# Layer normalisation moved from VectorE to ScalarE in a four-layer decoder, with a new table of step order

## The chip, the cores and the metric

The kernel is one program on one core of a Trainium2 chip. The time is the device time of that core in microseconds. The engines are named as in the profile: PE is the matrix engine (TensorE), PEld its weight loads, DVE is VectorE, ACT is ScalarE, POOL is GpSimd, SP is SyncE, which issues most of the DMAs.

## The reference

The reference is a decoder of 4 layers over x of shape (4, 256, 128) in float32: 4 batch entries, 256 tokens, width 128. Each layer is attention of some kind, cross attention of some kind and a feed-forward part with 8 experts; behind each of the 12 comes

```python
def _layernorm(x, axis=-1, eps=1e-05):
    m = jnp.mean(x, axis=axis, keepdims=True)
    v = jnp.var(x, axis=axis, keepdims=True)
    return (x - m) / jnp.sqrt(v + eps)

x = _layernorm(x + _L0_attn_ref(...))      # a state space scan over the tokens
x = _layernorm(x + _L0_xattn_ref(...))
x = _layernorm(x + _L0_ffn_ref(...))       # attention, rmsnorm, experts, rmsnorm inside
x = _layernorm(x + _L1_attn_ref(...))      # ... and so on, 12 times
```

The first feed-forward part holds an attention and two RMS normalisations with a weight vector of its own. The third feed-forward part (L2) sends tokens to experts through memory; the attention of L3 is linear attention with a softmax feature map.

## The kernel before, in words

The program calls the 12 parts 13 sublayers (`SUBLAYERS`), since the attention inside the first feed-forward part counts by itself as `("attn", 1)`. A sublayer is worked through for each of the 4 batch entries b. A batch entry is 256 tokens, held as two tiles of 128 tokens on the partitions by 128 features (`x_tok`), and also transposed (`xT`, features on the partitions), which is what the matmuls read.

All work is cut into some 2,550 steps, such as ("SM", a, b, i), ("P2", a, b, i) or ("NORM", s, b). A step names what it does on each engine; the tuple `COST` and the function `cost` give the planner's figures for it. `lanes()` puts the steps in 49 lanes, each with a fixed order within itself. The string `ORDER` has one letter for each step and says from which lane the next step comes. `plan()` reads it, chooses the PSUM banks, and puts in filler matmuls (step FILL, line 1036, on the identity matrix) where its own figures leave PE waiting for long. Each engine then goes through the steps in this one order and issues its own part of each. An engine's instructions run in the order in which they were issued; semaphores join the engines. So a step whose input is late holds up everything behind it on that engine.

At the end of a sublayer stand, for each batch entry, these steps:

- STAT: DVE adds the residual into `res` (line 1804), takes mean and variance with two BATCH_NORM_STATS2 and two BATCH_NORM_AGGREGATE (lines 1726 and 1730) into `mv`; POOL adds epsilon to the variance (line 1679) and raises it to the power -0.5 (line 1680) into `rstd`. STAT2 is a second such step in the first expert sublayer.
- NORM: DVE waits for `rstd` and computes (res - mean) * rstd, one TENSOR_SCALAR for each of the two tiles (line 1833). In `("attn", 1)`, which is an RMS normalisation, it is `res * rstd * norm_w` (line 1831). DVE then waits for its own result.
- XT: PE transposes `x_tok` (line 1062), ACT copies it to `xT` (line 1381). Everything in the next sublayer for that batch entry reads this.

Other names: line 1774 is the scan of the first sublayer on DVE, line 1371 the exponentials that it reads (ACT), 1377 a copy (ACT), 1611 the product behind it (POOL). Line 1448 is the exponential of the softmax (ACT), 1875 the row maximum (DVE), 1701 a product on POOL in the linear attention, 2012 the product with the gates in the expert parts (DVE).

The 13 sublayers of the 4 batch entries overlap in the order. Read by the lines that run in them, the stretches are roughly: to 134 us the scan of the first sublayer, to 275 us the first two attentions, to 560 us the first experts, the wide self attention, a cross attention and the second experts, to 700 us the causal and masked attentions, to 850 us the dispatched experts, to 1000 us the linear attention, then the last cross attention and the last experts.

Of the kernel before, what the change touches and what calls it, by code (L numbers as in the profile page):

```python
# [62 lines left out]
    "STAT": ((DVE, 1.2), (POOL, 1.1)), "XB": ((POOL, 0.8),), "STAT2": ((DVE, 1.95), (POOL, 1.1)), "NORM": ((DVE, 0.62),), "XT": ((PE, 0.22), (ACT, 0.33)),  # L63
# [31 lines left out]
def cost(st):  # L95
# [6 lines left out]
    if st[0] == "STAT":  # L102
        return ((DVE, 2.7 if SUBLAYERS[st[1]] == ("moe", DISPATCHED) else 1.55 if st[1] in RMS_SUBLAYERS else 1.2), (POOL, 1.1))
# [118 lines left out]
def needs(st, feats):  # L222
# [255 lines left out]
    "aaaacaadbccedcbcabebdcfdbffaadacacebeddcbcffeedbcdfbcfefbdceebbdfdccefeedbfbfddfcbcceefbbddfebdfeeecccffdbcdfbdbceedbfff"  # L478
    "bcefcbdedbdfeeeccdbfebcdfdfbfpcceeacdpbbpdafdbceedapcdnbbfceffeecabffffcqanqdbmeddcbqcdbceffbceduqeebfcdebcfbfddbedcfeec"
    "bcbdbcfebcddooohhhnvcffefebfhcfddhdebchheedfchbbiinbfofccddoebdefefhfeccbddbbjdffccjrceejehrdbbirffdbodefejfdcchbecrebbd"  # L480
    "cfnfdheiledohhcfnbcoldbbjjhfefeihdejfhfifjlsslhsmjjhsjphxonhhiinhpjhhlhpplhijgjgggoojpihphjnlohilmnjwojqmqjhijqlqhjlqjhh"
    "jhohjUlqvhhiohlnhirhhhiornjhjjhrjrlhiijlrojhrjjhinoouhlhjlnimjsmjhhsjhlhhisjsljhiojjshlhhhslonpmhiijphihnjpjjophlphhjljg"
    "hpijhpljoohyhiyyypylpthhhyyyhhijqhjmiqijzzjhqlhjlqAjhhAjjiAqlqittztzzzjjzlqAAjjrlAqrilrqjzwjAAjrjAAyltrpryplzzyyApsryytt"
    "tpsyyArsAxsspyrnmyszzzztAAyzzynztAAsAAAAmyoozsqmAAmqttostzqztqzmAyyyqyhhnmnyzzzAthhhhAAAAhAohihyryzyyymrAzzhzrroizymjjjA"
    "AztmzlrAjohhAlnihhnlAAzlAhhhohAimlAlsjsijllmmsomhhsojjillllslhhmnlllnjhimmpijjhmplhhjhlmooplmhhjomlnllliillThhhjmljhmmhi"
    "ihjjlllmhinhjlllllqljjlqjlmollllqhhhjnlljoojhnlllllihhhTmmmmooorhhhijmmmihirjjllmlrhihjjllljihnnlllljhjollolhjjlliljhljh"
    "jshmsjolihhijsljhnohhhliijnphhjmphjjplpihjlojphphjjpilhjljojqphjyihhtyyyhthizyhyzqyzzlhijAqqqljAjhtziAhjlqmljjhzAVrqAhii"
    "jjylrAtqylttjzjrzAAAtrtAjjlrpzyrAplpzyyysrpAsnysssyyrAyynztAoszzAAzzzzAzsAoAtoAyAyqqyqszztztyyzzyqAAnttoAzAhthhAntAAAAhy"
    "ryryyhyyruzrzoihhynnAzmhhAzyoiAjzhjhzzAzoAAihhjkkAoAAAhjsklvkhshijolsjhkkhjksiihjnmkhohlhihnljjpkkjhpjkkhhpplhijkljjphpi"
    "kkjkoohhnllimniqhojjhkqikhjojqkkwqhhlhjljkkjqhxihqjhkkhohnilmnhjihljrkkihjrjkkhlhrjjkrhlikjjjorjmhhoklrnhikhojhVjhlinhhs"  # L490
    "jjihhloshjholhsshjjsohSjilhsjvhlniompiimpjwnhhhhjjjhjhlpuppVlhhojhhjjjjoijlhlipqhihhqhpqjxjjljihqjhTlqjhhjjqjiliqlhirjBD"
    "mriTjjjljjljrDDjDjTrECFlEylrFryysrGysyHsGyysHGyyHsGyEFyHGIyysHyWEGEyGHsyyHFIyBDDDGyGHyFyHGyIyHDGyyHGyyHGyyHyGGHHEEIIJJJF"
    "CyyyJFGyyHGyEyHGpyypHqTGyyFHpyyqGKGKyHyIKKHGyyKKEHFGKyLLyHEGIFyyLHIGyyHGyyHLLGyyHLGyyLqHyMMMGGHHIIJJJJMMMMKKONNNNKLLOONN"
    "NNKNNOKPPPPTMMPPPPsLNQNNNNNNQLRQNrKRQPPPMPMNLKRrNPQPQPPLMNNNsLKNQQKROMrOPLRMLPNNPsNpPNKPpPppMpPppppPLKpNMMQpQNNNLNpKRNpQ"
# [96 lines left out]
def decoder(nc, I, scratch, gate_rows_out, lin_out, slots_in, slots_out, out):  # L591
# [15 lines left out]
    with ExitStack() as ctx:  # L607
# [3 lines left out]
        def sem(name):  # L611
            return ctx.enter_context(nc.semaphore(name))
# [1569 lines left out]
```

## Time and profile before

| | us |
|---|---|
| median of 3 runs | 1147.34 |
| lowest and highest | 1146.41, 1150.63 |
| the profiled execution | 1148.62 |
| its span (first to last instruction) | 1146.3 |
| PE busy | 1063.8 |
| DVE busy | 901.9 |
| ACT busy | 696.9 |
| POOL busy | 392.9 |

The span is what the trace covers. The profiled execution took 2.3 us more than its span, and is 1.3 us above the median. The busy times overlap each other, so they don't add up to the span. The granted clock of PE was 0.976 of its full 2.4 GHz on the mean over the span.

### The profile page before, as it was taken

What the parts mean: (1) busy time and instruction counts of PE and PEld (TensorE: products, weight loads), DVE (VectorE), ACT (ScalarE), POOL (GpSimd) and SP (SyncE); (2) the same over time, 40 slices, a digit from 0 to 9 for tenths busy, and PEclk for the clock granted to TensorE, in tenths of its full rate; (3) what the DMA queues carried; (4) which work ended last, traced back from release to release, by engine and by line L of the source; (5) the groups of instructions that cost most, each with busy time, mean ns of one, the idle gap of its engine ahead of it and who ended that gap; (6) DMA issues with size and microseconds to landing.
All of it is one profiled execution on the core that took longest, in us unless ns stands there. A gap on an engine that the chain in (4) does not pass through costs nothing. (4 is left out here: it accounts for less than half of the span.)

```text
span 1146.3 us, 24781 instructions
## 1 busy us (share of the span) xinstructions
PE 1063.8 (93%) x7996; PEld 691.3 (60%) x7996; DVE 901.9 (79%) x2409; ACT 696.9 (61%) x1554; POOL 392.9 (34%) x649
## 2 busy tenths in 40 slices
PE   6767898899999999999888999999999999999998
PEld 2433454567777875677544444665667676775676
DVE  6999977886888889667989862418899999878745
ACT  4555687875555558886664544446576556657662
POOL 4555433212221212122674433041475345421001
PEclk9888998999999999999889999999999999999999
DMA  8011243312422422224223424141100001132311
GB/s 273 1 54 49 65 130 105 121 40 86 125 69 82 119 70 85 95 81 143 90 83 106 165 76 186 33 136 45 32 29 1 1 20 42 61 103 60 105 43 51
DMA packets 75772, 93.54 MB, mean 82 GB/s; under 512 B 6520, under 2 KB 60256, under 8 KB 73696
## 3 DMA queue, kind: packets, MB, share of 16 engines
q1 hardware_dynamic: 74624, 89.86, 24.6%
q0 software_dynamic: 1024, 2.10, 0.6%
q8 instruction: 68, 1.11, 0.4%
q14 instruction: 56, 0.46, 0.1%
HBM read 64.78 MB, written 28.67 MB: 82 GB/s over the span
## 5 line engine op out<-in xcount | busy, mean ns | idle before, releaser
L1448 ACT ACTIVATE P<-bank 128x512 f32<-128x512 f32 (+1 forms) x448 | 229.6, 584 | 78.3 <-PE bank L1143 77.3
L1875 DVE TENSOR_REDUCE mx<-bank 128x2 f32<-128x512 f32 x320 | 198.9, 682 | 30.5 <-PE bank L1118 28.3
L1161 PE MATMUL bank<-P,V 128*32 128x256 f32 (+1 forms) x1536 | 101.9, 384 | 1.7 <-ACT P L1448 1.6
L1679 POOL TENSOR_SCALAR rstd<-mv 128x2 f32<-128x2 f32 x56 | 14.2, 253 | 248.5 <-DVE mv L1730 197.2
L1266 PE MATMUL bank<-room 128*128 128x256 f32 x384 | 96.6, 388 | 0.0
L1260 PE MATMUL bank<-xT,room 128*128 128x256 f32 x384 | 95.2, 387 | 0.1
L1118 PE MATMUL bank<-QKR 48*128 48x256 bf16 (+1 forms) x896 | 77.8, 270 | 15.7 <-DMA QKR<-split_rows 5.2
L1143 PE MATMUL bank<-QKR 50*128 50x256 bf16 (+1 forms) x896 | 80.4, 273 | 6.8 <-DVE mx L1875 2.5
L1622 POOL CAST ms<-mx 128x16 bf16<-128x16 f32 x56 | 14.8, 264 | 194.4 <-DVE mx L1875 166.4
L1260 PEld LDWEIGHTS bank<-xT,room 128*128 128x128 f32 x384 | 69.6, 190 | 16.5 <-issue 7.6
L1266 PEld LDWEIGHTS bank<-room 128*128 128x128 f32 x384 | 69.0, 190 | 15.0 <-issue 6.3
L2012 DVE TENSOR_TENSOR room<-room 128x512 f32<-128x512 f32 x96 | 66.7, 742 | 14.0 <-DMA room<-gate_rows 12.7
L1492 ACT ACTIVATE room<-bank,b 128x256 f32<-128x256 f32 x128 | 52.8, 471 | 24.4 <-PE bank L1260 23.7
L1118 PEld LDWEIGHTS bank<-QKR 48*128 48x128 bf16 x896 | 33.0, 94 | 55.4 <-issue 21.7
L1611 POOL TENSOR_TENSOR room<-room 128x256 f32<-128x256 f32 x64 | 48.4, 762 | 51.0 <-DVE room L1774 35.3
L1161 PEld LDWEIGHTS bank<-P,V 128*32 128x32 f32 x1536 | 41.5, 111 | 39.4 <-issue 16.3
L1171 PEld LDWEIGHTS bank<-room,P 128*128 128x128 f32 x512 | 60.4, 192 | 6.1 <-issue 4.5
L1171 PE MATMUL bank<-room,P 128*128 128x129 f32 x512 | 63.4, 278 | 0.0
L1143 PEld LDWEIGHTS bank<-QKR 50*128 50x128 bf16 x896 | 32.1, 95 | 50.1 <-issue 27.2
L1774 DVE TENSOR_TENSOR_SCAN room<-room 128x256 f32<-128x256 f32 x64 | 59.9, 935 | 2.2
L1240 PE MATMUL bank<-room 128*128 x120 | 58.3, 596 | 2.0 <-ACT room L1500 2.0
L1545 ACT ACTIVATE room<-room 128x512 f32<-128x512 f32 x50 | 28.8, 624 | 51.4 <-DVE room L2034 51.2
(281 smaller groups left out, 2426.8 us busy)
## 6 DMA issues: line engine op xcount, KB each, us to landing
QKR<-split_rows SPq DMA_DIRECT2D x112, 192.0 KB
room<-gate_rows SPq DMA_DIRECT2D x48, 256.0 KB, 3.6
split_rows<-parts SPq DMA_DIRECT2D x56, 192.0 KB, 2.3
split_rows<-parts SPq DMA_DIRECT2D x56, 128.0 KB, 2.2
room<-in_w SPq DMA_DIRECT2D x6, 1024.0 KB, 7.6
room<-in_w SPq DMA_DIRECT2D x3, 2048.0 KB, 8.9
split_rows<-parts SPq DMA_DIRECT2D x56, 64.0 KB, 1.9
room<-in_mask SPq DMA_DIRECT2D x4, 512.0 KB, 5.1
```

The lines of the kernel that those rows point to most:

```text
L1118: last = nc.tensor.matmul(psum(st, p)[:, t * S:t * S + nk], QKR[rows, buf, 0, i, t * 128:(t + 1) * 128], QKR[rows, buf, 1, i, 0:nk], start ...
L1143: last = nc.tensor.matmul(psum(st, p)[:, t * S:t * S + S - q0], QKR[rows, buf, 1, i, t * 128:(t + 1) * 128], QKR[rows, buf, 0, i, q0:S], s ...
L1161: last = nc.tensor.matmul(bk[32 * j:32 * j + 32, q0:S], V[:, n % 2, t, 8 * half + 4 * r + j, :], P[:, (e - 1 + j) % NBUF_P, t * S:t * S + ...
L1171: last = nc.tensor.matmul(bk[:, q * S:q * S + D + 1], P[:, (e - 1) % NBUF_P, t * S + q * 128:t * S + (q + 1) * 128], Z[:, b % 2, t, h, 0:D ...
L1240: last = nc.tensor.matmul(bk[:, :], x, w[:, bass.DynSlice(expert[j] * 512, 512)], start=True, stop=True)
L1260: last = nc.tensor.matmul(bk[:, j * S:(j + 1) * S], w1s[m][:, e, j * 128:(j + 1) * 128], xT[:, S * b:S * (b + 1)], start=True, stop=True)
L1266: last = nc.tensor.matmul(y[:, 0:S], w2s[m][:, e, j, :], hT[:, slot_of(b, e), j * S:(j + 1) * S], start=(m == 0 and (e, j) == (0, 0)), sto ...
L1448: nc.scalar.activation(P[:, (e - 1) % NBUF_P, 0:width], psum(st, p)[:, 0:width], ACT.Exp, scale=SCALE).then_inc(read[k], 1)
L1492: last = nc.scalar.activation(to[:, j * S:(j + 1) * S], bk[:, j * S:(j + 1) * S], ACT.Gelu if m == 1 else ACT.Relu, bias=b1[:, m // 2, e, ...
L1774: V_.tensor_tensor_scan(hs[:, at, :], abar[:, at, :], bu[:, at, :], 0.0, ALU.mult, ALU.add).then_inc(scan_done, 1)
L1875: V_.reduce_max(to, sc[:, :].rearrange("p (t s) -> p t s", t=TPB), AX.X).then_inc(read[k], 1)
L2012: V_.tensor_tensor(to, to, gb[:, e:e + 1, :].to_broadcast([128, 2, S]), ALU.mult).then_inc(scaled, 1)
```

## The change

NORM moves from DVE to ACT in 12 of the 13 sublayers: one ACTIVATE with the function Identity for each tile, which computes `res * rstd + centre` with `rstd` and `centre` as one number per token (partition). `centre` is -mean * rstd and is made by POOL in two more small operations within STAT and STAT2. The RMS normalisation of `("attn", 1)` stays on DVE with a semaphore of its own. Two semaphores change their use (`select_in` is gone, its two loads count on `lin_loaded`), and the waits on `norm_done` count tiles instead of steps. The planner's figures for the steps change, and `ORDER` is another string with the same steps.

```diff
-    "STAT": ((DVE, 1.2), (POOL, 1.1)), ... "STAT2": ((DVE, 1.95), (POOL, 1.1)), "NORM": ((DVE, 0.62),), ...
+    "STAT": ((DVE, 1.2), (POOL, 1.45)), ... "STAT2": ((DVE, 1.95), (POOL, 1.45)), "NORM": ((ACT, 0.6),), ...
...
+    if st[0] == "NORM" and SUBLAYERS[st[1]] == ("attn", 1):
+        return ((DVE, 0.62),)
...
-    "aaaacaadbccedcbcabebdcfdbffaadacacebeddcbcffeedbcdfbcfefbdceebbdfdccefeedbfbfddfcbcceefbbddfebdfeeecccffdbcdfbdbceedbfff"
+    "aaaacdaaccbbbddfccacebdfcebeffdbdefcbedbdccceedbffeedcbafbefdeabdccdbccbcfdfaeafbfdcefbdebdfeccbdfcedbfcfeebddbffefbcdeb"
...
                 elif k == "XT":
                     _, s, b = st
-                    pe.wait_ge(norm_done, count[("NORM", s, b)])
+                    pe.wait_ge(scaled_rows if SUBLAYERS[s] == ("attn", 1) else norm_done, TPB * norm_no(("NORM", s, b)))
...
+                elif k == "NORM" and SUBLAYERS[st[1]] != ("attn", 1):
+                    _, s, b = st
+                    act.wait_ge(rstd_done, stat_no[("STAT2" if SUBLAYERS[s] == ("moe", 0) else "STAT", s, b)])
+                    for t in range(TPB):
+                        nc.scalar.activation(x_tok[:, TPB * b + t, :], res[:, b, t, :], ACT.Identity, bias=centre[:, b, t:t + 1], scale=rstd[:, b, t:t + 1]).then_inc(norm_done, 1)
...
                     link(nc.gpsimd.tensor_scalar(rstd[:, b, :], mv[:, b, :, 1], RMS_EPS if rms else LN_EPS, None, ALU.add))
-                    nc.gpsimd.tensor_tensor(rstd[:, b, :], rstd[:, b, :], minus_half[:, :], ALU.pow).then_inc(rstd_done, 1)
+                    if rms:
+                        nc.gpsimd.tensor_tensor(rstd[:, b, :], rstd[:, b, :], minus_half[:, :], ALU.pow).then_inc(rstd_done, 1)
+                        continue
+                    nc.gpsimd.tensor_scalar(centre[:, b, :], mv[:, b, :, 0], -1.0, None, ALU.mult).then_inc(pool_chain, 1)
+                    chain[0] += 1
+                    link(nc.gpsimd.tensor_tensor(rstd[:, b, :], rstd[:, b, :], minus_half[:, :], ALU.pow))
+                    nc.gpsimd.tensor_tensor(centre[:, b, :], centre[:, b, :], rstd[:, b, :], ALU.mult).then_inc(rstd_done, 1)
...
-                elif k == "NORM":
+                elif k == "NORM" and SUBLAYERS[st[1]] == ("attn", 1):
                     _, s, b = st
-                    dve.wait_ge(rstd_done, stat_no[("STAT2" if SUBLAYERS[s] == ("moe", 0) else "STAT", s, b)])
-                    for t in range(TPB):
-                        x, r = x_tok[:, TPB * b + t, :], res[:, b, t, :]
-                        if SUBLAYERS[s] == ("attn", 1):
-                            last = V_.scalar_tensor_tensor(out=x, in0=r, scalar=rstd[:, b, t:t + 1], in1=norm_w[:, 0, :], op0=ALU.mult, op1=ALU.mult)
-                        else:
-                            last = V_.tensor_scalar(x, r, mv[:, b, t, 0:1], rstd[:, b, t:t + 1], ALU.subtract, ALU.mult)
...
-                    last.then_inc(norm_done, 1)
-                    dve.wait_ge(norm_done, count[st])
-                    dve.wait_ge(dve_chain, chain[0])
```

Three places show what stands in a row now. On DVE in the scan stretch, at the end of the first sublayer of the first batch entry, before (`room` holds the scan's inputs and outputs; 1769 is the product ahead of a scan, 1774 the scan):

```order
L1730 BN_AGGR mv<-stats 128x2
L1769 TENSOR_TENSOR room<-bank,room 128x256 [waits MB_filled]
L1774 SCALAR_TENSOR_TENSOR room<-room 128x256 [waits gated_done,abar_done,MB_read]
L1769 TENSOR_TENSOR room<-bank,room 128x256 [waits MB_filled]
L1774 SCALAR_TENSOR_TENSOR room<-room 128x256 [waits gated_done,abar_done,MB_read]
L1833 TENSOR_SCALAR x_tok<-res,mv,rstd 128x128 [waits rstd_done]
L1833 TENSOR_SCALAR x_tok<-res,mv,rstd 128x128
L1769 TENSOR_TENSOR room<-bank,room 128x256 [waits MB_filled,dve_chain,norm_done]
```

The same place on DVE now, where the two lines of the scan are 1791 and 1796:

```order
L1752 BN_AGGR mv<-stats 128x2
L1791 TENSOR_TENSOR room<-bank,room 128x256 [waits MB_filled]
L1796 SCALAR_TENSOR_TENSOR room<-room 128x256 [waits gated_done,abar_done,MB_read]
L1791 TENSOR_TENSOR room<-bank,room 128x256 [waits MB_filled]
L1796 SCALAR_TENSOR_TENSOR room<-room 128x256 [waits gated_done,abar_done,MB_read]
L1791 TENSOR_TENSOR room<-bank,room 128x256 [waits MB_filled]
```

The two TENSOR_SCALAR and the wait for `rstd_done` between two scans are gone, and no wait for DVE's own normalised tile stands ahead of the next product.

The second place is ACT at the same point of the program. Before (1371 the exponential that a scan reads, 1377 a copy that POOL's product reads, 1351 the start of the next batch entry's step widths, 1381 the copy of the transposed tile):

```order
L1371 ACTIVATE room<-room 128x256 [waits scan_done]
L1377 COPY room<-bank 128x256 [waits gated_done,MC_filled] x2
L1351 ACTIVATE room<-bank,room 64x256 [waits DT_filled]
L1377 COPY room<-bank 128x256 [waits gated_done,MC_filled]
L1371 ACTIVATE room<-room 128x256 [waits scan_done]
L1377 COPY room<-bank 128x256 [waits gated_done,MC_filled]
L1381 COPY xT<-bank 128x256 [waits XT_filled]
```

ACT now (1382, 1388, 1362 and 1397 are those lines, in the same roles):

```order
L1388 COPY room<-bank 128x256 [waits gated_done,MC_filled]
L1382 ACTIVATE room<-room 128x256 [waits scan_done]
L1393 ACTIVATE x_tok<-res,centre,rstd 128x128 [waits rstd_done]
L1393 ACTIVATE x_tok<-res,centre,rstd 128x128
L1388 COPY room<-bank 128x256 [waits gated_done,MC_filled]
L1362 ACTIVATE room<-bank,room 64x256 [waits DT_filled]
L1397 COPY xT<-bank 128x256 [waits XT_filled]
L1382 ACTIVATE room<-room 128x256 [waits scan_done]
```

The normalisation stands between the exponentials and copies of the scan, and the wait for `rstd_done` with it. The third place is POOL in the linear attention stretch, now (1723 is the long product, 1728 the causal cut):

```order
L1728 AFFINE_SELECT P<-P 128x2x128 [waits LA_read] x6
L1695 TENSOR_SCALAR rstd<-mv 128x2 [waits stat_done]
L1699 TENSOR_SCALAR centre<-mv 128x2 [waits pool_chain]
L1701 TENSOR_TENSOR rstd<-rstd,minus_half 128x2
L1702 TENSOR_TENSOR centre<-centre,rstd 128x2 [waits pool_chain]
L1723 TENSOR_TENSOR room<-room,lden 128x1024 [waits lsum_done]
```

Before, two operations stood there where there are four: the power, and the addition ahead of it. Of filler matmuls the program had 86 in 27 places (line 1036), and has 61 in 20 places (line 1047).

## Rows read from the trace of the kernel before

**Rows 1.** The page: the span, and the busy time of each engine.

```profile
span 1146.3 us, 24781 instructions
...
PE 1063.8 (93%) x7996; PEld 691.3 (60%) x7996; DVE 901.9 (79%) x2409; ACT 696.9 (61%) x1554; POOL 392.9 (34%) x649
```

**Rows 2.** Windows: us from:to and length, busy time of each engine, clock, DMA share, GB/s.

```profile
17.00:134.00 117.00, 89.79 (x450) 48.09 (x448) 112.61 (x197) 68.90 (x176) 63.41 (x89) 0.88 0.18 61
134.00:275.00 141.00, 128.77 (x1270) 76.64 (x1269) 110.81 (x299) 101.91 (x222) 35.90 (x78) 0.98 0.29 94
275.00:560.00 285.00, 278.76 (x2116) 200.88 (x2114) 235.51 (x726) 183.19 (x397) 69.61 (x137) 1.00 0.32 98
560.00:700.00 140.00, 126.38 (x1183) 63.12 (x1181) 109.32 (x526) 73.44 (x176) 68.25 (x136) 0.94 0.36 120
700.00:850.00 150.00, 144.34 (x792) 92.77 (x789) 87.45 (x176) 87.64 (x173) 49.91 (x52) 1.00 0.21 65
850.00:1000.00 150.00, 146.90 (x1076) 107.52 (x1074) 140.25 (x220) 90.25 (x201) 75.23 (x91) 1.00 0.08 23
```

**Rows 3.** Windows of line 1833 (DVE) alone: length, busy us (instructions), clock, DMA.

```profile
17.00:134.00 117.00, 3.67 (x6) 0.88 0.18 61
...
sum 1147.00, DVE 37.95; mean DVE 4.74
```

**Rows 4.** Waits from 17 to 134 us: engine, tile, line, releaser: us, times, longest.

```profile
POOL room L1611 <- DVE room L1774: 35.3, 36, 7.3
ACT room L1371 <- DVE room L1774: 27.0, 33, 2.0
```

**Rows 5.** Timeline of DVE at the first normalisation: start us, us, instruction.

```profile
63.48 0.69 DVE L1774 TENSOR_TENSOR_SCAN room<-room 128x256 f32<-128x256 f32 x1
64.09 1.37 DVE L1833 TENSOR_SCALAR x_tok<-res,mv,rstd 128x128 f32<-128x128 f32 x2
```

**Rows 6.** Line 1833 as a source: durations min/median/max, waits before it and on it.

```profile
L1833 DVE TENSOR_SCALAR x_tok<-res,mv,rstd x96: 254/344/1976, 64.1 to 1143.6; 128x128 f32<-128x128 f32 x96
...
  POOL rstd L1680: 19.2, 18
...
  PE bank L1062: 5.0, 7
```

**Rows 7.** Timeline near 948 us, all engines: a normalisation beside POOL.

```profile
947.72 2.30 DVE L1833 TENSOR_SCALAR x_tok<-res,mv,rstd 128x128 f32<-128x128 f32 x2
...
948.03 1.90 POOL L1701 TENSOR_TENSOR room<-room,lden 128x1024 f32<-128x1024 f32 x1
...
950.16 0.41 PE L1062 MATMUL bank<-ident,x_tok 128*128 128x128 f32 x2 [0.82 <-DVE x_tok L1833]
```

**Rows 8.** Groups of ACT by form: busy us, mean ns of one | idle before.

```profile
L1371 ACT ACTIVATE room<-room 128x256 f32<-128x256 f32 x64 | 32.1, 511 | 29.8 <-DVE room L1774 27.0 <-DVE room L1762 2.2
...
L1518 ACT COPY room<-bank 128x128 f32<-128x128 f32 x30 | 7.9, 264 | 9.0 <-PE bank L1251 9.0
...
L1360 ACT ACTIVATE room<-room 128x256 f32<-128x256 f32 x4 | 1.7, 417 | 0.1
```

**Rows 9.** Groups of POOL by form: the small operations.

```profile
L1680 POOL TENSOR_TENSOR rstd<-rstd,minus_half 128x2 f32<-128x2 f32 x56 | 42.6, 761 | 4.7
...
L1623 POOL TENSOR_TENSOR ms<-mx,ms 128x16 bf16<-128x16 f32 x56 | 15.3, 273 | 4.5
...
L1679 POOL TENSOR_SCALAR rstd<-mv 128x2 f32<-128x2 f32 x56 | 14.2, 253 | 248.5 <-DVE mv L1730 197.2 <-DVE mv L1738 51.2
```

**Rows 10.** Timeline of the end, all engines: POOL and DVE behind the last addition.

```profile
1142.62 0.71 POOL L1680 TENSOR_TENSOR rstd<-rstd,minus_half 128x2 f32<-128x2 f32 x1
1143.36 0.60 DVE L1833 TENSOR_SCALAR x_tok<-res,mv,rstd 128x128 f32<-128x128 f32 x2 [1.14 <-POOL rstd L1680]
```

**Rows 11.** Windows of line 1036 (filler matmuls) alone.

```profile
700.00:850.00 150.00, 7.30 (x27) 2.64 (x27) 1.00 0.21 65
```

**Rows 12.** Line 1774, the scan on DVE, as a source: durations min/median/max.

```profile
L1774 DVE TENSOR_TENSOR_SCAN room<-room x64: 691/1054/1071, 17.3 to 133.3; 128x256 f32<-128x256 f32 x64
```

More of the change, by code:

```diff
@@ L62 @@
     "MY": ((DVE, 0.9), (PE, 0.4)),
-    "STAT": ((DVE, 1.2), (POOL, 1.1)), "XB": ((POOL, 0.8),), "STAT2": ((DVE, 1.95), (POOL, 1.1)), "NORM": ((DVE, 0.62),), "XT": ((PE, 0.22), (ACT, 0.33)),
+    "STAT": ((DVE, 1.2), (POOL, 1.45)), "XB": ((POOL, 0.8),), "STAT2": ((DVE, 1.95), (POOL, 1.45)), "NORM": ((ACT, 0.6),), "XT": ((PE, 0.22), (ACT, 0.33)),
     "GQ": ((PE, 0.43), (ACT, 0.3)), "GS": ((PE, 0.43), (DVE, 1.7)), "GT": ((PE, 0.44), (ACT, 0.5)), "GM": ((PE, 0.86), (ACT, 0.3)),
@@ L102, in cost @@
     if st[0] == "STAT":
-        return ((DVE, 2.7 if SUBLAYERS[st[1]] == ("moe", DISPATCHED) else 1.55 if st[1] in RMS_SUBLAYERS else 1.2), (POOL, 1.1))
+        return ((DVE, 2.7 if SUBLAYERS[st[1]] == ("moe", DISPATCHED) else 1.55 if st[1] in RMS_SUBLAYERS else 1.2), (POOL, 1.45))
+    if st[0] == "NORM" and SUBLAYERS[st[1]] == ("attn", 1):
+        return ((DVE, 0.62),)
     if st[0] == "SM" and st[1] == MASKED:
@@ L482 @@
[L482 to L485, printed above, removed]
@@ L500 @@
+    "sssshhjWlhssoijljhjhshjlishhlnjpminopjjpjppnlhhlnijjnphhjnopyjlhihnylipohtththymyqjzyyzqyjjjqyAlotAhAqqzzzzlizhhhqiAhyyh"
+    "qzyAjijyAjhihAqtjlhhlyyrjhiArjjijrAyrtzztlAzzzrylrtjjArjjAlAlrzztAsAAzsysspzpyAsAAtttAAsyqsypyyyAysqyqzztAAyzzzAAyzzttzz"
+    "zytyzzAAyyzAAAyrrrAAAAAAzzAAAsss"
 )
@@ L626, in decoder @@
         rstd = sb("rstd", [128, B, TPB])
+        centre = sb("centre", [128, B, TPB])
         minus_half = sb("minus_half", [128, TPB])
@@ L844, in causal_before, with norm_no @@
             return 2 * split_maxima.index(st) + p + 1
+        row_scaled = [st for st in steps if st[0] == "NORM" and SUBLAYERS[st[1]] == ("attn", 1)]
+        normalised = [st for st in steps if st[0] == "NORM" and SUBLAYERS[st[1]] != ("attn", 1)]
+        def norm_no(st):
+            return (row_scaled if st in row_scaled else normalised).index(st) + 1
         def head_no(st, p):
@@ L970, in _ @@
                             full(sp, ("ZV", B - 1, NH - 1))
-                            sp.wait_ge(norm_done, max(count[("NORM", SUB_OF[("moe", 0)], b)] for b in range(B)))
+                            sp.wait_ge(norm_done, TPB * max(norm_no(("NORM", SUB_OF[("moe", 0)], b)) for b in range(B)))
                         load(w1s[m], f"w1_{m}", experts_in)
@@ L992, in _ @@
                     full(sp, ("DO", 1, NBLOCK - 1))
-                    load(select, "select", select_in)
-                    load(one_of, "one_of", select_in)
+                    load(select, "select", lin_loaded)
+                    load(one_of, "one_of", lin_loaded)
                 elif st[:2] == ("LD", "ctx"):
@@ L1001, in _ @@
                     b = st[2]
-                    sp.wait_ge(norm_done, count[st])
+                    sp.wait_ge(norm_done, TPB * norm_no(st))
                     sp.dma_start(out[b].rearrange("(t p) d -> p t d", p=128),
@@ L1312, in _ @@
                     pe.wait_ge(masked, B * NH + count[("LA", b, 4 * r + 3)])
-                    pe.wait_ge(select_in, 32)
+                    pe.wait_ge(lin_loaded, 16 * N_LIN + 80 + 32)
                     y = psum(("LN", b))
```

44 lines of the change are left out of this document (23 added, 21 removed).

## The prediction

> **What bounds the kernel now.** I read the page first, for the span and the busy times, then the windows by stretch, then everything about the moved line 1833, then the price of the operations that replace it. PE is busy 1063.8 of 1146.3 us [rows 1], so about 82.5 us of idle PE is all that any reordering can win. The windows say where that is [rows 2] (their busy columns are PE, PEld, DVE, ACT, POOL). From 17 to 134 us, the scan stretch, PE is busy 89.8 of 117 us, and idle for 27.2; DVE is busy 112.6, thus 96%, and ACT and POOL wait for DVE's scan, 27.0 and 35.3 us [rows 4]. There DVE sets the pace. From 134 to 275 us PE is idle 12.2 us of 141, with DVE busy 110.8 and ACT 101.9: no engine is alone the bound. From 275 to 560 us PE is idle 6.2 of 285 us and is the bound. From 560 to 700 us it is idle 13.6 of 140, with DVE busy 109.3. From 700 to 850 it is idle 5.7 of 150. From 850 to 1000 us PE is idle 3.1 and DVE is busy 140.3 of 150, so both are nearly full. The rest of the 82.5 us lies in the first 17 us and behind 1000 us, where PE ends before the last additions.
>
> So time taken off DVE counts in full only in the scan stretch, in part up to 275 us and from 560 to 700 us, and nearly nowhere else.
>
> **What goes from DVE.** 96 TENSOR_SCALAR with 37.95 us busy in all [rows 3], and a wait for POOL's `rstd` that left DVE idle 18 times, 19.2 us in all [rows 6]. Six of the 96 stand in the scan stretch, with 3.67 us busy [rows 3]; the first pair stands between two scans and takes 1.37 us [rows 5]. Around them nothing else changes on DVE, as the order shows: the same products and scans. DVE has 4.4 us of idle in that stretch, none of it named for this line, so I count 3.7 us less for the end of the scans. It could be nothing, if a scan then waits for ACT's exponentials (a normalisation now stands among them), and not more than 3.7 plus what the idle gives; I put the ends at 0 and -5.
>
> POOL does two more operations for each of 48 normalisations, and they may stand against DVE. A scan takes 691 ns at the least and 1054 at the median [rows 12], and 0.69 us where it runs without much POOL work beside it [rows 5]. Line 1833 took 2.30 us for two near 948 us, while POOL's long product ran 1.90 us [rows 7], against a median of 344 ns each [rows 6]. The Trainium skill (GPSIMD Engine Reference, 1. Specifications) says that POOL and DVE share their SBUF interface and contend when DVE has two SBUF inputs or uses its two-port mode. By this rule, with which the stretched rows agree, the long waits of the moved operation vanish, and the two new POOL operations can hold up a scan. If each of three pairs held a scan by one operation's 0.27 us twice, the scan stretch would gain 3.7 - 1.6 = 2.1 us instead of 3.7.
>
> **What comes to ACT.** No ACTIVATE of 128x128 with two numbers per partition stands in the trace. From below: the copy of 128x128, without them, takes 264 ns [rows 8]. An ACTIVATE from SBUF with 256 columns and no such operand takes 417, one with a scale per partition 511 [rows 8], so an operand costs 94 ns, and the upper end is 417 + 2 x 94 = 605, as if half the columns saved nothing. I take 264 + 2 x 94 = 452, since 128 columns are what the copy has, thus 0.9 us for a pair, where DVE needed 0.60 [rows 10]. For 96 that is 43 us more on ACT, 740 of 1146 us, 65%. The planner's figure of 0.6 for the pair is 0.3 too low. ACT is not the bound anywhere in [rows 2], so the busy time is hidden behind PE; if the cover goes, it is 0.3 us for each pair.
>
> **What comes to POOL.** In STAT one operation like line 1679, 253 ns, and one like line 1623, 273 ns [rows 9], and by my estimate 0.04 of hop for each: 0.6 us more between `mv` and the release of NORM. The planner was given 0.35 (1.1 to 1.45), so it is 0.25 too low. The power itself, 761 ns [rows 9], stays.
>
> **The latency of a normalisation** thus grows by 0.6 + 0.3 = 0.9 us, of which the new table knows about 0.35. PE waited for `x_tok` 7 times before, 5.0 us in all [rows 6]; elsewhere the transpose had slack. If the seven are late by the 0.55 us that the planner doesn't know, that is +3.9, and as many places again with less slack may join. Against this the pairs held up by POOL go: the one near 948 us took 1.6 us over the usual 0.69, and PE waited 0.82 us for it [rows 7]. I take +1.5 us in sum, with ends of -3 and +8.
>
> **At the end** nothing hides the chain. POOL 0.71, hop, DVE 0.60, DMA [rows 10]. It grows by the full latency: +0.9 us, with ends of +0.5 (if the copy's price holds for ACT) and +1.2 (at 605 ns).
>
> **The two middle stretches.** From 134 to 275 us DVE loses its pairs and the waits ahead of them, and PE has 12.2 us to win. I take a quarter, -3 us, ends 0 and -6. From 560 to 700 us PE has 13.6 us to win, pairs leave DVE again, and the order is new; I take -2, ends +2 and -5. Both are by choice between nothing and about half of the idle time, nearer to nothing, since PE there waits for several engines in turn.
>
> **The new step table** has 61 filler matmuls where there were 86. From 700 to 850 us, where PE is nearly the bound, 27 of them took 7.30 us [rows 11], 0.27 each; the new program has 23 in the corresponding part. That is -1 us. The others mostly stood in the scan stretch, where PE is idle anyway, and cost nothing; what they may do for the clock (0.88 in that stretch [rows 2]) I can't price, and PE is not the bound there. Where steps swap places inside PE-bound stretches, I count nothing, ends -4 and +4. The two loads that now count on `lin_loaded` come before what reads them by a long way: nothing.
>
> **Sum**, against the profiled execution: -3.7 - 3 - 2 - 1 + 1.5 + 0.9 = -7.3 us, 1148.62 to 1141.3 us. That execution is 1.3 us above the median of the runs, 1147.34, so a median of 1140.0 us.
>
> **Rivals.**
>
> *ACT becomes the gate (slower).* Each NORM now stands in ACT's queue and waits for POOL; the softmax exponentials (line 1448), whose output PE reads and whose PSUM banks it needs, are queued behind it. Place: from 134 to 700 us, where ACT is busiest. DVE waited 18 times, 1.07 us on average [rows 6]; ACT would wait as often with 0.6 more, 30 us idle. For: the latency that the planner underrates by 0.55 us in each of 48 steps. Against: ACT was idle a third of the time, and exponentials are mostly ahead of need in PE-bound stretches. It decides from the point where more than about 13 us of the 30 reach PE: 7.3 us of gain eaten and 5.7 above. With half of the 30, it is 1140.0 + 15 = 1155 us.
>
> *The gain is hidden (no change).* DVE's relief is real, but PE is the bound nearly everywhere, and the scan stretch gives its 3.7 us while late transposes take 3 and the end 0.9. Then the time is 1147.3 + 0.2, thus 1147.5 us. For: PE busy 93%. Against: 27.2 us of idle PE in the scan stretch, where DVE alone is full.
>
> *The new table does much more than the move.* A table that was looked for with another set of costs can also reach PE's idle time between 134 and 700 us that has nothing to do with NORM, 12.2 + 6.2 + 13.6 = 32.0 us. With half of it gone, and the scan's 3.7 and the end's 0.9: 1147.3 - 16 - 3.7 + 0.9 = 1128.5 us. For: 25 fewer fillers, which the planner puts only where it sees PE wait. Against: it moves steps in small ways, and most stretches stand as they were.
>
> **How the numbers follow.** Two medians of this kernel can be told apart from about 0.5%, 5.7 us, so faster means below 1141.6 and slower above 1153.1. Forecast, 1135 to 1145: 0.47. Hidden, 1145 to 1152: 0.27. Much more, below 1135: 0.14. ACT as the gate, above 1152: 0.12. Of the forecast's own range a good half lies under 1141.6, about 0.33 of the 0.47, and with the 0.14 faster gets 0.48 and something for the unequal weight of its middle: 0.50. Slower gets the 0.12 less what lies under 1153.1, plus a little for a table that is plainly worse: 0.13. The same: 0.37. The range holds 8 of 10 when it leaves about 0.1 at either side: from 1131 to 1153. The sum of all the ends would be wider, but they would not fall on one side together.
>
> **What would show it.** In the changed profile: the last scan starts near 129.6 instead of 133.3 us; ACT's line 1393 has 96 of about 0.45 us; between the power on POOL and the last normalisation stands a product of about 0.27 us; DVE is busy some 38 us less and waits for `rstd` only in the eight steps that need it there; the stretches from 275 us on keep their PE share. The forecast would be wrong if PE's waits for `x_tok` (line 1073 or so) were above 10 us, or ACT's exponentials were late behind NORM, or if the scans ended as late as before.

## The result and the profile after

The changed kernel took 1154.01 us at the median of 15 runs (1150.67 to 1156.94), the kernel before, in 15 runs beside it, 1148.14 us (1143.41 to 1153.86). The ratio is 1.0053, with a 95% interval of 1.0037 to 1.0068. So in these runs the change made the kernel slower by about half a per cent; 1140.0 us was forecast, and the time lies 1 us above the range. A second set of runs on another chip, below, gave 0.9985 [0.9961, 1.0009]. The two sets don't agree on the sign of so small a difference, but neither shows the gain of 7.3 us.

The profiled execution of the changed kernel took 1153.69 us. Its page, beside [rows 1]:

```profile
span 1151.9 us, 24773 instructions
...
PE 1060.6 (92%) x7962; PEld 690.0 (60%) x7971; DVE 867.2 (75%) x2313; ACT 732.6 (64%) x1652; POOL 415.6 (36%) x745
```

DVE lost 34.7 us, ACT gained 35.7, POOL 22.7. PE is busy 3.2 us less, and idle 91.3 us instead of 82.5. The windows of the same stretches, to be held beside [rows 2] (stretch and length, then PE, PEld, DVE, ACT, POOL busy, clock, DMA share, GB/s):

```profile
17.00:134.00 117.00, 91.31 (x476) 51.42 (x474) 110.18 (x196) 72.68 (x187) 67.42 (x97) 0.90 0.22 73
134.00:275.00 141.00, 127.78 (x1241) 74.00 (x1238) 107.64 (x286) 105.68 (x231) 37.74 (x88) 0.96 0.27 83
275.00:560.00 285.00, 275.96 (x2094) 200.22 (x2094) 219.75 (x684) 192.26 (x421) 69.92 (x159) 0.99 0.33 105
560.00:700.00 140.00, 124.10 (x1153) 61.72 (x1160) 105.96 (x522) 77.88 (x190) 72.65 (x153) 0.93 0.27 88
700.00:850.00 150.00, 142.17 (x785) 90.25 (x784) 82.22 (x155) 87.52 (x173) 49.57 (x53) 1.00 0.24 81
850.00:1000.00 150.00, 146.65 (x1066) 108.09 (x1064) 138.66 (x219) 96.21 (x216) 78.91 (x107) 1.00 0.08 25
```

Only the scan stretch has less idle PE than before (25.7 against 27.2 us). In the next five PE idles 1.0, 2.8, 2.3, 2.2 and 0.2 us more, 8.5 in all, though DVE has less to do in each. The edges stand still while the work moves by a few us, so this is a map, not an account.

The moved operation as a source, and the product on POOL that releases it, to be held beside [rows 6]:

```profile
L1393 ACT ACTIVATE x_tok<-res,centre,rstd x96: 477/490/562, 61.1 to 1149.2; 128x128 f32<-128x128 f32 x96
...
  POOL centre L1702: 23.4, 20
...
  PE bank L1073: 5.2, 9
```

```profile
L1702 POOL TENSOR_TENSOR centre<-centre,rstd x48: 194/195/722, 60.8 to 1148.6; 128x2 f32<-128x2 f32 x48
```

No ACTIVATE lasted over 562 ns, where DVE's version had reached 1976. The Trainium skill (ScalarE: Activation LUTs, What ACT_TABLE_LOAD costs) has a formula for an ACTIVATE; worked out for two pointer operands and 128 columns, it gives an estimate of 479 ns. The trace agrees, with 477 ns at the least and 490 at the median.

The end, all engines, to be held beside [rows 10]:

```profile
1145.49 0.44 PE L1283 MATMUL bank<-ident,yT 128*128 128x128 f32 x2
...
1146.95 0.25 DVE L1752 BATCH_NORM_AGGREGATE mv<-stats 128x2 f32<-128x6 f32 x2
1147.29 0.22 POOL L1695 TENSOR_SCALAR rstd<-mv 128x2 f32<-128x2 f32 x1 [5.71 <-DVE mv L1752]
1147.59 0.22 POOL L1699 TENSOR_SCALAR centre<-mv 128x2 f32<-128x2 f32 x1
1147.77 0.71 POOL L1701 TENSOR_TENSOR rstd<-rstd,minus_half 128x2 f32<-128x2 f32 x1
1148.55 0.20 POOL L1702 TENSOR_TENSOR centre<-centre,rstd 128x2 f32<-128x2 f32 x1
1148.78 0.88 ACT L1393 ACTIVATE x_tok<-res,centre,rstd 128x128 f32<-128x128 f32 x2 [3.34 <-POOL centre L1702]
```

From the first operation on POOL to the start of NORM it is 1.49 us, where it was 1.05 (1142.31 to 1143.36 before), and the pair lasts 0.88 instead of 0.60: the chain grew by 0.7 us. The last transposes of the expert output, which start at 1145.49 here, started at 1140.52 before:

```profile
1140.52 0.44 PE L1272 MATMUL bank<-ident,yT 128*128 128x128 f32 x2
```

So 5.0 of the 5.6 us of longer span were lost ahead of the tail. With the 48 normalisations of each kernel paired in order of time, 13 of the 16 up to 440 us end earlier than before, by up to 7.5 us. Of the 26 from 538 us on, 23 end later, most of them by 1 to 8 us. So the early lead is lost between about 440 and 540 us.

### The profile page after: what moved, and what is told of

The parts are those of the page before. It is cut to its first block and busy times, and to the rows that moved or that the text cites. A ratio compares the mean times of both kernels' runs of the same rounds, so it can differ in the third digit from the quotient of the medians.

```text
span 1151.9 us, 24773 instructions
## 1 busy us (share of the span) xinstructions
PE 1060.6 (92%) x7962; PEld 690.0 (60%) x7971; DVE 867.2 (75%) x2313; ACT 732.6 (64%) x1652; POOL 415.6 (36%) x745
## 5 line engine op out<-in xcount | busy, mean ns | idle before, releaser
L1695 POOL TENSOR_SCALAR rstd<-mv 128x2 f32<-128x2 f32 x56 | 16.7, 299 | 229.6 <-DVE mv L1752 189.5
L1129 PE MATMUL bank<-QKR 48*128 48x256 bf16 (+1 forms) x896 | 80.4, 277 | 10.9 <-ACT P L1464 3.6
L2025 DVE TENSOR_TENSOR room<-room 128x512 f32<-128x512 f32 x96 | 62.9, 698 | 16.4 <-DMA room<-gate_rows 13.8
L1711 POOL TENSOR_TENSOR qk<-qk,parts 128x256 f32<-128x256 f32 x56 | 38.2, 703 | 90.1 <-ACT parts L1433 90.1
L1172 PEld LDWEIGHTS bank<-P,V 128*32 128x32 f32 x1536 | 42.1, 111 | 39.2 <-issue 14.3
L1880 DVE CUSTOM_DVE_ANT_0 room<-bank,room 128x256 f32<-128x256 f32 x128 | 49.2, 421 | 18.5 <-PE bank L1129 16.8
```

The source lines that it names most:

```text
L1129: last = nc.tensor.matmul(psum(st, p)[:, t * S:t * S + nk], QKR[rows, buf, 0, i, t * 128:(t + 1) * 128], QKR[rows, buf, 1, i, 0:nk], start ...
L1172: last = nc.tensor.matmul(bk[32 * j:32 * j + 32, q0:S], V[:, n % 2, t, 8 * half + 4 * r + j, :], P[:, (e - 1 + j) % NBUF_P, t * S:t * S + ...
L1880: last = V_.tensor_tensor_reduce(out=unused[:, t, 0:nk], in0=sc[:, t * S:t * S + nk], in1=to_add, scale=1.0, scalar=-3e38, op0=ALU.add, op ...
L2025: V_.tensor_tensor(to, to, gb[:, e:e + 1, :].to_broadcast([128, 2, S]), ALU.mult).then_inc(scaled, 1)
```

## The experiments

**The changed kernel again**, as the base for the runs beside it.

> The changed kernel again, beside the others on one chip. It should stand at 1.0053 of the kernel before, and shows how far such a ratio moves from chip to chip. If it came out under 1.002, the loss that the others are to explain would be one of the chip and not of the change.

Measured: 1156.33 us, before 1158.45, ratio 0.9985 [0.9961, 1.0009]. By the mark set above, under 1.002, the half per cent of the first set is not a loss that can be put down to the change alone. What all sets leave to explain is why the gain is missing.

**The move alone, with the old table.** Instructions as in the changed kernel; `ORDER`, `COST`, and so banks and fillers, as before. The lines are shown against the changed kernel.

```diff
-    "STAT": ((DVE, 1.2), (POOL, 1.45)), ... "NORM": ((ACT, 0.6),), ...   # and the new ORDER
+    "STAT": ((DVE, 1.2), (POOL, 1.1)), ... "NORM": ((DVE, 0.62),), ...   # and the old ORDER
```

> The move alone: normalisation on ScalarE with the shift by POOL, but the step table, the planner's costs, the banks and the fillers of the kernel before, so that PE's instructions are word for word those of before. Theory A (the new table is what costs; the move itself gains the 3.7 us of the scan stretch and gives back 1 at the end): 0.997 to 0.999. Theory B (the move costs: the normalisation waits in ScalarE's queue, its chain is 0.9 us longer, and transposes and exponentials behind it are late): 1.005 or more. Under B the waits of PE for x_tok and for ACT's exponentials must be more than the 5.0 us of before for x_tok.

Measured: 1200.72 us, 1.0366 [1.0326, 1.0405]. Its waits (engine, tile, line, releaser: us, times, longest):

```profile
ACT x_tok L1391 <- POOL centre L1700: 47.1, 22, 5.3
...
PE bank L1071 <- ACT x_tok L1391: 14.7, 14, 2.0
...
PE bank L1170 <- ACT P L1462: 5.4, 3, 3.5
```

ACT stands 47.1 us in front of NORM, twice as long as with the new table, and PE waits 14.7 us for `x_tok` (5.0 in [rows 6]). PE also waits for exponentials, `P`, which come from ACT's queue too: 16.2 us summed over its lines, against 6.1 before and 8.8 in the changed kernel. These are the waits that the rival "ACT becomes the gate" names. They are not the whole of the 42 us: in the profiled executions PE is idle 115.4 us instead of 82.5, and busy 1079.8 us instead of 1063.8 with the same matmuls, at a mean granted clock of 0.964 instead of 0.976. Some 33 us are waits, and some 16 are slower matmuls (the kernel before was profiled in another set of runs). Why the clock is lower is open.

**The table alone, normalisation on DVE.** The changed kernel's head with the engine parts of before.

```diff
+    (the new ORDER and COST)
                 elif k == "NORM":
                     dve.wait_ge(rstd_done, ...)   # as before
```

> The table alone: the new step table with its costs, banks and fillers, PE's instructions word for word those of the changed kernel, but the normalisation on VectorE as before, with no shift from POOL. Theory A (the table costs): 1.005 or more, as slow as the changed kernel or slower. Theory B (the move costs): 0.997 to 1.001.

Measured: 1190.13 us, 1.0278 [1.0232, 1.0325]. The wait that pays for it:

```profile
PE bank L1064 <- DVE x_tok L1835: 22.4, 15, 4.3
```

In an order made for another queue, PE waits 22.4 us for the tile that DVE normalises, where it was 5.0. Both of the marks set above (1.005 or more) are met at once: table and move each cost 30 to 40 us alone and nearly nothing together, so neither "the table costs" nor "the move costs" was the right question.

**The changed kernel without the shift.** One operation behind the addition on POOL instead of three. This kernel leaves out the subtraction of the mean.

```diff
-    nc.scalar.activation(..., ACT.Identity, bias=centre[...], scale=rstd[...])
+    nc.scalar.activation(..., ACT.Copy, scale=rstd[...])
-    (tensor_scalar into centre, and the product centre * rstd, on POOL)
```

> The changed kernel with the shift left out: the two POOL operations for it are gone and ScalarE multiplies by rstd alone (the mean is not subtracted, which is left out of the computation). The chain from statistics to the normalised tile is then about 0.5 us shorter (measured in the changed kernel: 0.22 and 0.20 us on POOL, two hops of 0.08, and about 0.09 on each ACTIVATE). Theory B (length of the chain costs): a good half of the loss goes, 1.000 to 1.003, 3 us or more under the changed kernel. Theory A (the table costs, wherever its steps stand): 0.6 us at the end and little more, 1.004 to 1.005.

Measured: 1151.75 us, 0.9952 [0.9925, 0.9979], beside 0.9985 for the whole change on the same chip: 4.6 us between the two medians. Its waits, to be held beside those of the changed kernel:

```profile
ACT x_tok L1393 <- POOL rstd L1699: 12.8, 9, 2.9
...
PE bank L1073 <- ACT x_tok L1393: 2.2, 4, 1.0
```

ACT's wait fell from 24.5 us (22 times, changed kernel on this chip) to 12.8. ACT was also busy 7.8 us less (724.4 against 732.2), so the 4.6 us are the price of the shift as a whole. Between the means of the two it is 4.6 us, with a 95% interval of 2.3 to 6.9.

**The shift without the move.** The kernel before, with the two operations put into the chain; NORM on DVE waits for them and doesn't use them.

```diff
+    nc.gpsimd.tensor_scalar(centre[:, b, :], mv[:, b, :, 0], -1.0, None, ALU.mult).then_inc(pool_chain, 1)
+    link(nc.gpsimd.tensor_tensor(rstd[:, b, :], rstd[:, b, :], minus_half[:, :], ALU.pow))
+    nc.gpsimd.tensor_tensor(centre[:, b, :], centre[:, b, :], rstd[:, b, :], ALU.mult).then_inc(rstd_done, 1)
```

> The kernel before, with the two POOL operations for the shift put in but not used: the normalisation stays on VectorE and starts 0.5 us later, everything else is word for word as before. It prices the length of the chain alone under the table of before. Theory C (a table is fitted to the durations; every start that comes later than it allows is paid again and again, since the queues are in order): of the 42 us that the move cost under this table, a third or more, 1.012 or above. Theory D (the place of the work in ScalarE's queue is what costs, not the chain): 1.001 to 1.005. What I forecast before any run would give 0.5 us at the end and some 4 us on transposes, 1.004.

Measured: 1154.23 us, 1.0037 [1.0013, 1.0061], thus 4.3 us.

```profile
DVE x_tok L1840 <- POOL centre L1687: 31.6, 30, 1.6
...
PE bank L1063 <- DVE x_tok L1840: 6.8, 9, 1.2
```

DVE waits 30 times instead of 18, and 31.6 us instead of 19.2 [rows 6]. With ACT left alone, the two POOL operations cost about what the shift costs in the changed kernel. The profiled execution is the slowest of the 12 (1158.01 us), so its waits are rather those of a bad run. The result lies in the range set for theory D and at the 1.004 that the first forecast would have given, not at theory C's 1.012.

**The move with the old table and without the shift.**

```diff
-    (the move alone, above) ACT.Identity, bias=centre[...], scale=rstd[...]
+    ACT.Copy, scale=rstd[...]
```

> The move under the old table, with the shift left out (the mean is not subtracted): the normalisation is on ScalarE, and its release comes as early as before. What is left is the wait of 23 more us in ScalarE's queue and the 0.3 us by which the pair takes longer. Theory C: much of the 1.037 goes, 1.015 to 1.025. Theory D: little goes, 1.030 or more.

Measured: 1168.45 us, 1.0167 [1.0123, 1.021]. Where the order doesn't fit, the same half microsecond in 48 chains costs 2.0% (1.0366 to 1.0167), not 0.3%. The two ratios are from two chips, between which a ratio can move by some 0.7% (the changed kernel's did), so the size is rough. Under the old table, then, theory C holds for the kernel with the move and theory D for the one without it.

**The changed kernel with the old `ORDER` and the new `COST`**: the sequence of before, banks and fillers by the new figures.

```diff
-    "aaaacdaaccbbbddfccacebdf...   (new ORDER)
+    "aaaacaadbccedcbcabebdcfd...   (old ORDER)
```

> The changed kernel with the string of step order of before; the planner's costs, and so the PSUM banks and fillers that it chooses, follow the new costs. Beside the move under the old table (1.037, whose banks and fillers are those of before) it tells whether banks and fillers matter. If the order of steps is what fits: 1.03 to 1.04, the same. If the banks were what did not fit: clearly less, 1.02 or below.

Measured: 1174.30 us, 1.0214 [1.0176, 1.0252]. Of the 3.7% of the move alone, 1.5 are gone with the new banks and fillers, and the rest goes with the new sequence (again across two chips). That is between the two outcomes named above. ACT still waits 49.0 us for `centre`; PE's matmuls wait less for `x_tok`:

```profile
PEld bank L1073 <- ACT x_tok L1393: 7.2, 7, 1.3
PE bank L1073 <- ACT x_tok L1393: 6.9, 12, 0.8
```

It isn't all won time. The plan puts in 144 filler matmuls here where the move alone has 86, busy 39.8 us instead of 26.4, so part of a former wait is filled and only the weight load still waits. PE is idle 93.3 us instead of 115.4. The mean clock of the runs is 0.975 here and 0.962 in the move alone; banks, fillers and clock were not told apart.

**The move in the scan stretch alone**, with the old table: the four normalisations of the first sublayer on ACT, all others on DVE.

```diff
+ON_ACT = (0,)
-                elif k == "NORM" and SUBLAYERS[st[1]] != ("attn", 1):
+                elif k == "NORM" and st[1] in ON_ACT:
```

> The old table, with the four normalisations behind the scan sublayer on ScalarE (and POOL's shift for them) and the other 48 on VectorE as before. This is the step of my forecast that took 3.7 us off the scan stretch, by itself. By the forecast: 0.996 to 0.998. By Theory C the earlier scans help, but ScalarE's exponentials and copies for the scan wait behind the normalisation: 1.000 to 1.005, with the last scan no earlier than 1 us before that of the kernel before.

Measured: 1152.99 us, 1.0019 [0.999, 1.0047]. The last scan started at 135.4 us, against 133.3 before [rows 12]. Alone, with the old table, the part of the forecast that looked safest gives nothing. ACT stood 8.5 us in four waits for `centre`, what it does next came later, and DVE's products ahead of the scans then waited for PE (4.7 and 2.6 us, where before it was 1.6):

```profile
DVE room L1792 <- PE bank L1060: 4.7, 4, 1.6
DVE room L1774 <- PE bank L1055: 2.6, 1, 2.6
```

That ACT's delay reaches PE and from there DVE is inferred from the order of these waits; no run isolates it.

**New tables, for both kernels.** A fitted table is part of what was timed, so both kernels were given others. Each is a new `ORDER`, found by an equally long search with the planner's own figures, and the banks and fillers that `plan()` makes of it; four of them also tell the planner 0.9 us for the pair on ACT, which measures 0.88, where the change says 0.6.

```diff
-    "NORM": ((ACT, 0.6),)
+    "NORM": ((ACT, 0.9),)   # and another ORDER
```

Moved, with 0.9, first table:

> The changed kernel with its step table looked for once more, with one figure set right: the planner is told 0.9 us for the pair of normalisations on ScalarE (measured 0.88) where the changed kernel tells it 0.6. If the wrong figure was what ate the gain (Theory E): 0.990 to 0.996 of the kernel before, and under the control that was looked for equally long with 0.6. If any further search gains alike, it stands level with the control, whatever its value.

Moved, with 0.6:

> The control: the changed kernel with a table looked for equally long, but with the 0.6 us. Theory E: 0.3% or more above the table with the right figure. Otherwise level with it.

The kernel before, first new table:

> The kernel before (normalisation on VectorE, nothing of the change) with a table looked for equally long. If the move has a value of its own once the tables are equally good, this one is slower than the changed kernel with its new table; if PE's work is what bounds both, the two are level within 0.3%, and the move is worth nothing.

Moved, with 0.9, second table:

> A second table for the changed kernel with the 0.9 us, from another start of the same search. It shows how far two tables of the same quality by the planner lie apart on the chip: with nothing else changed, I expect 0.3% at most. If they lie 0.5% or more apart, no difference of that size between kernels with different tables can be put down to the move.

Third and fourth, and two more of the kernel before:

> The changed kernel with a third new table, looked for as long as the others and with 0.9 us for the pair of normalisations on ACT. So far the changed kernel had 1.0053, 1.006, 1.0047 and 0.9966 of the kernel before with four tables, the kernel before 0.9965 with one new table. If the move is worth nothing and the table decides within half a per cent, this lies at 0.995 to 1.007. If the move costs 0.5% with any table: 1.003 to 1.007, and the 0.9966 was a lucky table. If a right figure for ACT makes the move pay: below 0.997.

> As the run with the third table, with a fourth: 0.995 to 1.007 if the table decides, 1.003 to 1.007 if the move costs with any table, below 0.997 if the move pays once its figure is right.

> The kernel before, normalisation on DVE, with a second new table, looked for equally long. If the table decides within half a per cent: 0.992 to 1.004, no better in the mean than the moved kernels. If the move costs 0.5% with any table: 0.994 to 0.999, as its first new table (0.9965), and clearly below the mean of the moved ones.

> The kernel before with a third new table: 0.992 to 1.004 if the table decides, 0.994 to 0.999 if the kernel before is the better one with any table looked for this long.

The two best, side by side on one chip:

> The changed kernel with the fourth new table once more (six runs so far, 0.987 of the kernel before, with an interval of 0.9829 to 0.9911). If that table is truly the best of all: 0.984 to 0.992 again, and below the kernel before with its own new table beside it. If the six runs were a draw from favourable ones: 0.994 to 1.002.

> The kernel before with its first new table once more, on the same chip as the moved kernel with the fourth: 0.994 to 0.999 as before (0.9965). If the moved kernel with its best table is better than the kernel before with its best, this lies at least 0.4% above it.

Measured:

| kernel, table | median us | before there | ratio |
|---|---|---|---|
| moved, 0.9, first | 1156.28 | 1148.85 | 1.0060 [1.004, 1.0079] |
| moved, 0.6 | 1152.99 | 1148.85 | 1.0047 [1.0018, 1.0075] |
| moved, 0.9, second | 1145.03 | 1148.85 | 0.9966 [0.9931, 1.0001] |
| before, first new | 1146.28 | 1148.85 | 0.9965 [0.9938, 0.9993] |
| moved, 0.9, third | 1164.29 | 1156.94 | 1.0058 [1.003, 1.0086] |
| moved, 0.9, fourth | 1142.68 | 1156.94 | 0.9870 [0.9829, 0.9911] |
| before, second new | 1154.94 | 1156.94 | 0.9969 [0.9942, 0.9997] |
| before, third new | 1159.59 | 1156.94 | 1.0013 [0.9988, 1.0039] |
| moved, 0.9, fourth, again | 1149.44 | 1160.67 | 0.9907 [0.9872, 0.9941] |
| before, first new, again | 1148.45 | 1160.67 | 0.9913 [0.9878, 0.9949] |

Four tables with the same figures and steps lie between 0.987 and 1.006. By the traces their instructions differ only in the fillers (53 to 66 matmuls) and in how often ACT loads an activation table (24 to 28 times, 1.28 us each). Expected were 0.3% at most between two such tables; the first and the second, on one chip, lie 0.9% apart.

Averaged by table, the moved kernel has 1.0007 over six (the one of the change among them, as the mean of 1.0053 and 0.9985, and the fourth as the mean over its 18 runs; standard error 0.0027, from their spread), the kernel before 0.9980 over four (1 for its own; 0.0017). The difference, 0.0027 with an error of 0.0032, is none that can be told. Side by side the best moved one and the best of before are level, both 0.9% faster than the kernel before; there the 0.4% that I expected between them if the move paid is missing (the means differ by 0.1 us, with a 95% interval of 3.3 either way). So the runs show no value of the move once each side has a good table. By twice the error, anything from a gain of 0.4% to a loss of 0.9% stays open. The right figure is no cure either: with 0.9 there are two tables slower and two faster than before, and the first of them is not faster than its control with 0.6 (1156.28 and 1152.99 us), where 0.3% or more was expected.

The idle time of PE in the profiled executions says the same with less of the clock in it. Where one kernel was profiled on two chips, it differs by 0.1, 1.3 and 3.0 us (first new table of before, the change, the fourth table). By table it is 92.0, 88.8, 92.7, 88.9, 98.4 and 82.7 us for the moved kernel, in the order change, first, 0.6, second, third, fourth, and 82.5, 86.5, 93.3 and 93.4 us for the kernel before. The means are 90.6 and 88.9 us.

The waits for the normalised tile in the two best, the moved one first:

```profile
ACT x_tok L1393 <- POOL centre L1702: 23.7, 20, 3.3
...
PE bank L1073 <- ACT x_tok L1393: 4.1, 4, 2.1
```

```profile
DVE x_tok L1833 <- POOL rstd L1680: 9.8, 11, 1.2
...
PE bank L1062 <- DVE x_tok L1833: 2.9, 5, 1.1
```

The engine that holds NORM waits more than twice as long when it is ACT, PE hardly more for the tile. Their busy times differ by 40.5 us on DVE (858.6 and 899.1) and 1.7 on PE (1062.0 and 1060.3), in spans of 1146.2 and 1146.7 us. The relief on DVE does reach PE's waits, and is eaten there: summed by what released them, PE's matmuls wait 21.9 us for DVE in the moved kernel and 34.1 in the other, but 21.3 instead of 16.6 for ACT, 17.7 instead of 14.8 for POOL and 10.4 instead of 8.8 for DMAs.

## Why the prediction was wrong

**The scans** were to gain 3.7 us. Their last one starts at 131.3 instead of 133.3 us:

```profile
L1796 DVE TENSOR_TENSOR_SCAN room<-room x64: 690/1054/1116, 18.2 to 131.3; 128x256 f32<-128x256 f32 x64
```

That is 2.0 us. The 2.1 that I had worked out for scans held up by POOL, and not taken, fits by chance only: the scans are busy 59.08 us instead of 59.49. I had also misread [rows 5]: the scan of 0.69 us at 63.48 did have POOL beside it, with the power until 63.65 and a product from 63.62 on, so it shows nothing of scans left alone. Most of the rest went into DVE's waits for PE, from 17 to 136 us:

```profile
DVE room L1791 <- PE bank L1059: 2.3, 4, 0.7
DVE res L1824 <- PE bank L1068: 1.3, 2, 0.8
```

They were 1.6 and 0.8 us before. The move alone with the old table had its last scan at 130.8 us, the scan-only run with the same table at 135.4: in this stretch most of the gain can be had, or all of it lost.

**The two middle stretches** were to gain 3 and 2 us, and this is the step that failed. I took "a quarter" of PE's idle time "by choice" where DVE was busiest, as if what a freer DVE releases stayed won, and put nothing for what PE would come to wait for on ACT. PE idles 1.0 and 2.3 us more in them. The waits of PE's matmuls, summed by the engine that released them (us, before and after), show what took the place of the gain:

| stretch | for DVE | for ACT | for DMA |
|---|---|---|---|
| 134 to 275 | 4.3, 1.7 | 3.4, 7.6 | 4.0, 3.0 |
| 275 to 560 | 3.8, 1.2 | 1.4, 6.3 | 0, 1.2 |
| 560 to 700 | 8.4, 7.3 | 4.6, 6.0 | 0, 0 |
| 700 to 850 | 0.9, 3.4 | 4.5, 2.7 | 0, 1.3 |

In the two middle stretches together the waits for DVE fell by 3.7 us, not far from the 5 forecast, and those for ACT rose by 5.6; with the stretch between them it is 6.3 less and 10.5 more. So the relief was real, and what PE then waited for on ACT took it back. The two best kernels, each picked from several tables, point the same way: 12.2 us less wait for DVE, 4.7 more for ACT, the same span. How much of the shift between the engines is the new order and how much the move, no run tells apart.

**Swaps inside PE-bound stretches** were counted as nothing, with ends of 4 us. From 275 to 560 us PE idles 2.8 us more, from 700 to 850 us 2.2. In the first of them ACT is the releaser: the exponentials `P`, the normalised tile and its transposed copy `xT`. PE's waits from 275 to 560 us in the changed kernel:

```profile
PE bank L1103 <- ACT xT L1397: 2.1, 1, 2.1
PE bank L1073 <- ACT x_tok L1393: 2.1, 3, 1.2
PE bank L1129 <- ACT P L1464: 1.9, 2, 1.3
```

Before, in the same stretch, no matmul waited for `P`, and the other two were

```profile
PE bank L1092 <- ACT xT L1381: 1.0, 1, 1.0
PE bank L1062 <- DVE x_tok L1833: 1.0, 2, 0.7
```

From 700 to 850 us, the dispatched experts, it is not ACT, but `room` of DVE (0.9 us before) and a load. The changed kernel has there:

```profile
PE bank L1256 <- DVE room L2032: 2.7, 3, 1.3
PE bank L1243 <- DMA room<-slots_in: 1.3, 1, 1.3
```

So the rival "ACT becomes the gate" names the right mechanism from 134 to 700 us, at a smaller size than its 15 us once the table is fitted, and at more than that when it isn't.

**The longer latency** was taken at +1.5 us in sum, the 4 us of the late transposes less what the stretched pairs give back. The wait of PE for `x_tok` is as long as it was, 5.2 us; the latency is paid where ACT or DVE stands in front of NORM and later work queues behind. The runs price the shift at 4.3 us with NORM on DVE and 4.6 us in the changed kernel, each on one chip, for 0.5 of the 0.9 us that I had as the whole latency. About 0.5 us of either is the end, which had a term of its own, so some 4 us stand against the 1.5: the term was 2 to 3 us short. Without the shift the changed kernel has 0.9952 on its chip, 5.5 us of gain against 7.3 forecast. On the chip of the first set, where the whole change had 1.0053, which is 6 us slower, the same 4 to 5 us would still leave it 1 to 2 us slower (an estimate), so a free shift alone doesn't bring the forecast gain.

**The account**, a rough one, since the edges of the windows stand still. By the stretches, the scans fall 1.7 us short, the middle ones 8.3 (5 forecast, 3.3 lost), the PE-bound ones 5.0. That makes 15.0, less the 1.5 that the sum held for late transposes, and less 2.2 us of PE's 3.2 less busy (the fillers' 1 was counted): 11.3 of the 12.4 us between 1141.3 and the profiled 1153.7. It says where the time is, not what a table of other luck would have made of it.

**Single prices** were right or close: ACT 0.49 us (forecast 0.45), the product 0.195 us (0.27), the end +0.7 us (0.9), DVE 34.7 us less (38), the fillers from 700 to 850 us 5.94 us where they were 7.30 [rows 11]. Wrong was "0.25 too low" for the planner's chain on POOL: it was told 1.45 us, and from 1147.29 to 1148.75 it is 1.46. By planner and trace the pair on ACT was the only one of these figures out of place.

**The table.** The forecast gave it a rival of its own for doing much more, 1128.5 us, and no term for a table that is as good or bad as chance made it. Its measured spread, 1.9% or 22 us from best to worst with the same steps (1.5% if the fourth table has its second ratio), is larger than any term of my sum and as wide as my whole range of 1131 to 1153 us. For that reason, too, I think the chance of slower, 0.13, was too small.

## What to carry to other kernels

When a change comes with a re-fitted order, don't judge the move by the old order, or the order by the old code: here these cost 3.7 and 2.8% alone, and say little of the pair. Give both sides several orders before a half per cent is put down to the move. Time moved from one in-order queue to another moves PE's waits with it: here those for DVE fell and those for ACT rose. So a forecast needs a term for what the receiving queue holds up, beside the one for what the freed engine releases. And half a microsecond added to a chain in front of an in-order queue is paid 48 times in small parts: 4.3 us in all under the order of the kernel before.

## What the runs showed of the hardware

- The time of one and the same kernel follows the granted clock of PE. In its 12 later runs the moved kernel with the fourth table went from 1140.23 us at a mean clock of 0.980 to 1154.57 us at 0.963. The first table had 0.967 on the mean of its runs and the second 0.977; at that slope of 14.3 us for 0.017 this is, as an estimate, 8 to 9 of the 11 us between them. Their profiles put all of it there: PE is idle 88.8 and 88.9 us, and busy 1067.3 us at 0.963 and 1053.2 at 0.977, in spans of 1156.1 and 1142.1 us. Orders of the same steps thus also differ by the clock that they are granted; why was not settled. Within the 12 runs of the first table alone, whose clocks lie between 0.963 and 0.971, time and clock hardly go together.
- The kernel before itself had medians of 1148.1, 1149.6 and 1148.9 us in some sets of runs and 1156.9, 1158.5 and 1160.7 in others, on other chips. The ratio of the same pair moves too: 0.9965 and 0.9913 for one kernel, 1.0053 and 0.9985 for another, more than their intervals in the second case. An interval within one set of runs doesn't cover that.
- Small POOL operations are stretched as well at times. The addition on 128x2 took 0.57 us at 1139.48, beside two DVE products of 128x512 that ran from 1139.31 to 1140.57, of which the second is shown, and 0.22 at the end with DVE idle:

```profile
1139.48 0.57 POOL L1695 TENSOR_SCALAR rstd<-mv 128x2 f32<-128x2 f32 x1 [14.52 <-DVE mv L1752]
...
1139.88 0.68 DVE L2025 TENSOR_TENSOR room<-room 128x512 f32<-128x512 f32 x1
```
